# Three batch-1 projections in front of the first attention pass, and a new order in SyncE's queue

## The chip, the cores and the metric

One core of a Trainium2 chip runs the whole program. The metric is device time in microseconds, the median of several executions. TensorE's clock has two levels, 1.2 and 2.4 GHz; the profile gives the granted share of full speed, 0.50 or 1.00.

## The reference

The input is `x` of shape (4, 512, 512): four batches of 512 rows. What is computed, with all else cut:

```
x = x + attention(layernorm(x))        # 32 query heads and 8 key heads of 16 features
x = x + ffn(layernorm(x))              # 1376 hidden features
attention: q, k, v = x@Wq, x@Wk, x@Wv; q, k = rope(q), rope(k)
           probs = softmax(causal(q k^T / 4)); out = (probs v) @ Wo
ffn:       (silu(x @ W_gate.T) * (x @ W_up.T)) @ W_down.T
```

All of it is float32.

## The kernel before

The kernel has two phases. Phase 1 does attention for the four batches, in four passes over one batch each; phase 2 does the rest, mostly the feed-forward matmuls. The change is in phase 1.

**A pass.** Pass `b` has eight groups, one for each key head with its four query heads. A group is numbered `n = 8*b + g` and has four slots, `i` = 0 to 3, for four row tiles or key chunks. In each slot TensorE, by `iteration`, interleaves three things step by step, the steps being `(i, j)`: the transposed scores of group `n` (`scores_t`, L1222), from which ScalarE makes the exponentials (L792); the plain scores of group `n+2` (`scores`, L1188, with a mask matmul at L1195), from which VectorE takes row maxima (L929 and L934) out of a ring of three PSUM banks `ps_s`; and the product of masked probabilities and values (`weighted_v`, L1235). The row maxima are split by GpSimd (L682, L684), transposed by TensorE at the end of slot 0 (`transposed_max`, L1206), copied to `m_t` by ScalarE (L785) and sent by SyncE into two rows of `q_rows` (`stage_max`, L465). The first `scores_t` of the next group waits for that transfer.

**Dense units.** Between these steps TensorE computes the next batch's projections, one unit after another in the PSUM bank `ps_d`. A unit of kind R is one of five projections (k=0 the keys, 1 to 4 the queries) and V is the values; each has four pieces of three matmuls of 512 columns (`project`, L1140). U transposes the values, T transposes the normalised rows of the batch after. Each pass has 40 places for a piece, five in a group, given by `gap(n)`; `UNITS_IN` says at which place a unit starts, and its pieces take consecutive places. `dense_evacuated` counts units read out of their bank. ScalarE copies an R unit to `raw` (`raw_rows`, L729, L730 and L743: three copies for k=0, one for the others), GpSimd rotates it in 20 steps at the slots of `ROPE_SLOT` (L595, L599), ScalarE and GpSimd write the bf16 parts (L753, L610) at `LO_SLOT`, and SyncE stores them to scratch (`store_rotated`, L405 and L409). From there `stage_rows` (six transfers, L452 and L455) loads a group's rows into a ring of six.

**The preamble.** Before pass 0 TensorE computes all projections of batch 0, then the transposes of batch 1, then the plain scores of groups 0 and 1. `transposed_max(0)` stands after the first slot of group 1. VectorE takes these maxima with L934.

**SyncE** issues all its transfers in program order and blocks at each wait. In slot `i` of a group it goes through: a rotated store (when the slot before is in `LO_SLOT`), the rows of group `n+3` (`i` = 0), the maxima of group `n+1` (`i` = 1), the output of group `n-1` (`i` = 2), and in pass 0 a 688 KB copy of a weight matrix within DRAM (`copy_raw`, `i` = 2 and 3).

**The end of phase 1.** In the last pass `LAST_O` gives two outputs `ps_o` to VectorE instead of ScalarE (L986), at slots 26 and 30. In a slot VectorE does this work before that of `LAST_XT` (L979, L901).

## Time and profile before

| what | value |
|---|---|
| median of 3 runs | 773.6 us (773.15 to 775.04) |
| the profiled execution's own time | 772.49 us |
| its span | 770.8 us |
| mean granted TensorE clock | 0.989 |
| TensorE busy | 737.8 us, 96% of the span |
| VectorE, ScalarE, GpSimd busy | 445.2, 333.8, 241.9 us |
| preamble up to the first `scores_t` | 53.4 us |
| phase 2 from | 369.6 us |

The span runs from the first to the last instruction; the execution's own time has 1.7 us more. Matmuls are pipelined, so that a busy TensorE row ends later than its columns do: the distance from start to start is the better measure of a matmul.

### The profile page before, as it was taken

How to read it: one execution, taken by the hardware profiler on the slowest of the kernel's cores; microseconds unless marked ns; L12 is line 12 of the kernel's file. 1: busy time of each engine (PE TensorE's matmuls, PEld its weight loads, DVE VectorE, ACT ScalarE, POOL GpSimd, SP SyncE). 2: the span in 40 equal slices, each digit the busy share in tenths (PEclk: the TensorE clock that was granted, in tenths of full speed). 3: DMA queues.
4: the chain of work that ended last, by engine and by line, in shares of the span. 5: the costliest groups of instructions: out<-in, count | busy, mean ns of one | idle time of the engine just before them, and what ended most of it. 6: DMA issues, size and time to landing. Idle time of an engine off the chain costs nothing.

```text
span 770.8 us, 12186 instructions
## 1 busy us (share of the span) xinstructions
PE 737.8 (96%) x4149; PEld 502.4 (65%) x4164; DVE 445.2 (58%) x1136; ACT 333.8 (43%) x646; POOL 241.9 (31%) x467
## 2 busy tenths in 40 slices
PE   5889999999999999998999999999999999999998
PEld 4645444554444543443788888888888888788886
DVE  6897789888987889997355443234232333231212
ACT  4337678767976778667343222111121111111111
POOL 4257885688658774556000000000000000000000
PEclk9869999999999999999999999999999999999999
DMA  7337587234434455530592103211014020030001
GB/s 272 98 108 250 182 280 239 67 87 125 119 96 130 142 179 151 160 99 29 174 310 72 42 14 118 88 59 51 14 48 142 27 82 27 0 110 1 1 0 55
DMA packets 74759, 81.86 MB, mean 106 GB/s; under 512 B 8864, under 2 KB 58528, under 8 KB 74496
## 3 DMA queue, kind: packets, MB, share of 16 engines
q1 hardware_dynamic: 73408, 79.98, 32.7%
q10 hardware_dynamic: 1296, 1.18, 0.5%
q8 instruction: 30, 0.49, 0.3%
q14 instruction: 25, 0.20, 0.1%
HBM read 57.02 MB, written 33.36 MB: 117 GB/s over the span
## 4 chain that ended last, share of the span: by engine, by line
PE 51%; DVE 0%; issue 0%; DVEq 0%
PE bank L1578 35%; PE ps_y L1630 15%; PE bank L1617 1%; DVE x_in L1560 0%; DVEq L1559 0%
## 5 line engine op out<-in xcount | busy, mean ns | idle before, releaser
L929 DVE CUSTOM_DVE_ANT_0 ps_s<-ps_s,mask_row 128x512 f32<-128x512 f32 (+1 forms) x360 | 192.1, 583 | 36.6 <-PE ps_s L1188 34.0
L792 ACT ACTIVATE probs<-ps_t 128x512 f32<-128x512 f32 (+1 forms) x352 | 178.2, 560 | 68.6 <-PE ps_t L1222 68.3
L1535 DVE TENSOR_TENSOR h<-h,bank 128x512 f32<-128x512 f32 (+1 forms) x44 | 30.2, 687 | 212.8 <-PE bank L1578 211.6
L1188 PE MATMUL ps_s<-k_rows,q_rows 96*128 96x256 bf16 (+3 forms) x512 | 141.0, 309 | 5.7 <-DVE m_raw L929 2.9
L1222 PE MATMUL ps_t<-q_rows,k_rows 98*128 98x512 bf16 (+1 forms) x352 | 126.9, 364 | 4.4 <-DMA q_rows<-m_t 2.4
L240 POOL TENSOR_TENSOR var_eps<-mean_var,eps 128x1 f32<-128x1 f32 x16 | 3.0, 189 | 281.7 <-DVE mean_var L235 281.7
L1473 ACT ACTIVATE h<-bank 128x512 f32<-128x512 f32 (+1 forms) x44 | 26.3, 597 | 145.2 <-PE bank L1578 145.2
L1235 PE MATMUL ps_o<-probs,v_ones 128*32 128x512 f32 (+3 forms) x1024 | 82.0, 438 | 3.4 <-POOL probs L693 1.1
L693 POOL TENSOR_SCALAR_AFFINE_SELECT probs<-probs 128x512 f32<-128x512 f32 x128 | 83.4, 652 | 0.0
L1479 ACT CAST h_hi<-h 128x512 fp32r<-128x512 f32 (+1 forms) x44 | 27.3, 620 | 126.5 <-DVE h L1535 126.5
L1188 PEld LDWEIGHTS ps_s<-k_rows,q_rows 96*128 96x128 bf16 x512 | 48.2, 100 | 47.8 <-DVE m_raw L929 22.3
L1630 PE MATMUL ps_y<-wd_hi,h_hi 128*128 128x512 f32 (+1 forms) x176 | 68.8, 391 | 0.0
L1222 PEld LDWEIGHTS ps_t<-q_rows,k_rows 98*128 98x128 bf16 x352 | 34.2, 98 | 53.1 <-issue 18.3
L1630 PE MATMUL ps_y<-wd_lo,h_hi 128*128 128x512 f32 (+1 forms) x176 | 68.5, 389 | 0.0
L1630 PE MATMUL ps_y<-wd_hi,h_lo 128*128 128x512 f32 (+1 forms) x176 | 68.5, 389 | 0.0
L1235 PEld LDWEIGHTS ps_o<-probs,v_ones 128*32 128x32 f32 x1024 | 27.2, 109 | 43.3 <-issue 30.4
L691 POOL TENSOR_TENSOR carrier<-half 128x1 f32<-128x1 f32 x128 | 26.8, 209 | 89.9 <-ACT probs L792 89.8
L929 DVE DVE_READ_ACCUMULATOR2_ANT m_raw<- 128x1 f32 x360 | 50.3, 140 | 0.0
L1578 PE MATMUL bank<-xt_hi,wg_hi 128*128 128x512 f32 (+1 forms) x128 | 50.0, 390 | 0.0
L1578 PE MATMUL bank<-xt_hi,wg_lo 128*128 128x512 f32 (+1 forms) x128 | 49.9, 390 | 0.0
L1578 PE MATMUL bank<-xt_hi,wu_lo 128*128 128x512 f32 (+1 forms) x128 | 49.9, 390 | 0.0
L1578 PE MATMUL bank<-xt_lo,wu_hi 128*128 128x512 f32 (+1 forms) x128 | 49.9, 390 | 0.0
(167 smaller groups left out, 1366.1 us busy)
## 6 DMA issues: line engine op xcount, KB each, us to landing
scratch_o<-o_sb SPq DMA_DIRECT2D x31, 256.0 KB, 2.4
q_rows<-scratch_q_parts SPq DMA_DIRECT2D x32, 192.0 KB
x_in<-in_x SPq DMA_DIRECT2D x16, 256.0 KB, 4.0
q_rows<-scratch_q_parts SPq DMA_DIRECT2D x32, 128.0 KB
o_in<-scratch_o SPq DMA_DIRECT2D x64, 64.0 KB
inverse<-scratch_inverse SPq DMA_DIRECT2D x64, 64.0 KB
x_res<-in_x SPq DMA_DIRECT2D x16, 256.0 KB, 2.7
out<-x_in SPq DMA_DIRECT2D x16, 256.0 KB, 2.1
```

Of the source, the lines that this page charges most:

```text
L691: nc.gpsimd.tensor_tensor(carrier[:, g % 2, c:c + 1], half[:, 0:1], half[:, 0:1], ALU.add)
L693: nc.gpsimd.affine_select(out=diagonal, in_=diagonal, compare_op=ALU.is_ge, fill=0.0, base=0, pattern=[[0, GROUP], [1, P]], channel_multip ...
L792: nc.scalar.activation(probs[:, g % 2, heads * u:heads * (u + 1), CHUNK_AT[c]:CHUNK_AT[c + 1]], ps_t[:, pos % S_BANKS, 0:heads * CHUNK_N[c ...
L929: taken = nc.vector.tensor_tensor_reduce(out=head, in0=head, in1=mask_row[:, T - width:T], scale=1.0, scalar=LOWEST, op0=ALU.add, op1=ALU. ...
L1188: mm = nc.tensor.matmul(bank[:, place], q_rows[r][0:ROWS, j, P * q:P * (q + 1)], k_rows[r][0:ROWS, 0:width], start=(place == 0), stop=(mas ...
L1222: nc.tensor.matmul(ps_t[:, pos % S_BANKS, 0:heads * width], k_rows[r][:, P * c:P * (c + 1)], q_rows[r][:, heads * u:heads * (u + 1), P * c:T],
L1235: mm = nc.tensor.matmul(ps_o[32 * j:32 * j + 2 * DH, P * c:T], v_ones[:, c, g % NKV, :], probs[:, g % 2, j, CHUNK_AT[c]:CHUNK_AT[c + 1]], ...
L1473: nc.scalar.activation(h[0:m, r], bank[units["gate", f] % BANKS][0:m, :], ACT.Silu).then_inc(silu_done, 1)
L1479: nc.scalar.copy(h_parts[0][0:m, r], h[0:m, r]).then_inc(h_hi_ready, 1)
L1535: nc.vector.tensor_tensor(h[0:m, r], h[0:m, r], bank[units["up", f] % BANKS][0:m, :], ALU.mult).then_inc(h_ready, 1)
L1578: mm = nc.tensor.matmul(out, weights(w, c), moving(m, c), start=(c == 0 and n == 0), stop=(c == chunks - 1 and n == 2))
L1630: mm = nc.tensor.matmul(ps_y[:, t], h_parts[w][0:m, r, P * t:P * (t + 1)], wd[p][0:m, f, :], start=(f == 0 and k == 0), stop=(f == FT - 1 ...
```

## The change

Three of the five R units of batch 1 (k = 0, 1, 2) are computed in the preamble, their twelve pieces between the scores of groups 0 and 1 (`AHEAD_AT`), in the banks `ps_t[2]`, `ps_d` and `ps_o`. Pass 0 keeps R3, R4 and V, whose pieces now take every second place, and U and the T units. ScalarE's copies of the first three units stand in the preamble, the first of them ahead of the first group's maxima; GpSimd does the four key steps of the rotation there. SyncE sends the maxima first at `i` = 1, stores rotated parts one slot later, and loads rows of group `n+4` at `i` = 3 instead of `n+3` at the next `i` = 0. `LAST_O` moves one output from slot 30 to slot 29. `transposed_max(0)` uses `ps_t[0]` and semaphores of its own.

```diff
-        steps = [gap(first + n) for n in range(1 if kind in "TU" else 4)]
+        steps = [gap(first + n) for n in ((0,) if kind in "TU" else range(0, 4 * apart[0], apart[0]) if apart else range(4))]
...
+AHEAD = 3
+AHEAD_AT = {(0, 1, 1): (0, 0), (0, 1, 3): (0, 1), (0, 2, 1): (0, 2), (0, 2, 3): (0, 3),
+            (1, 0, 1): (1, 0), (1, 0, 3): (1, 1), (1, 1, 1): (1, 2), (1, 1, 3): (1, 3),
+            (1, 2, 1): (2, 0), (1, 2, 3): (2, 1), (1, 3, 1): (2, 2), (1, 3, 3): (2, 3)}
+FIRST_UNITS = [("R", 3, 2, 2), ("R", 4, 11, 2), ("V", 0, 19, 2), ("U", 0, 27)]
+UNITS_IN = [FIRST_UNITS + NEXT_T] + [QKV_UNITS + NEXT_T] * (B - 3) + [QKV_UNITS, LAST_UNITS]
...
+FIRST_ROPE = [None] * ROPE_AHEAD + [1, 2, 3, 5, 6, 7, 9, 10, 13, 14, 15, 17, 18, 19, 21, 22]
-LO_SLOT = {7: 0, 13: 1, 16: 2, 23: 3, 27: 4}
+LO_SLOT = [{1: 0, 9: 1, 13: 2, 21: 3, 25: 4}] + [{7: 0, 13: 1, 16: 2, 23: 3, 27: 4}] * (B - 2)
-LAST_O = {26: 5, 30: 6}
+LAST_O = {26: 5, 29: 6}
...
-                    if has_next and slot - 1 in LO_SLOT:
-                        store_rotated(sp, b + 1, LO_SLOT[slot - 1])
-                    if i == 0 and n + 3 < GROUPS:
-                        stage_rows((n + 3) // NKV, (n + 3) % NKV, n + 3)
+                    if n == 0 and i == 0:
+                        stage_rows(0, 3, 3)
                     if i == 1 and n + 1 < GROUPS:
                         stage_max(n + 1)
+                    if has_next and slot - 2 in LO_SLOT[b]:
+                        store_rotated(sp, b + 1, LO_SLOT[b][slot - 2])
                     if i == PV_EVACUATE and n >= 1:
                         store_o(b, g - 1)
+                    if i == 3 and n + 4 < GROUPS:
+                        stage_rows((n + 4) // NKV, (n + 4) % NKV, n + 4)
...
             store_rotated(act, 0, 3)
+            raw_rows(1, 0, r_unit(1, 0))
             rotated_top(0, 4)
             first_max_high()
             max_evacuate(0)
             store_rotated(act, 0, 4)
+            for k in range(1, AHEAD):
+                raw_rows(1, k, r_unit(1, k))
...
                     for j in range(GROUP):
                         scores(0, n, i, j)
+                        if (n, i, j) in AHEAD_AT:
+                            k, piece = AHEAD_AT[n, i, j]
+                            dense(1, "R", k, r_unit(1, k), piece)
                     if (n, i) == (1, 0):
                         transposed_max(0)
```

## Rows read from the trace of the kernel before

**Rows 1.** The page: busy time by engine, and the chain that ended last.
```profile
PE 737.8 (96%) x4149; PEld 502.4 (65%) x4164; DVE 445.2 (58%) x1136; ACT 333.8 (43%) x646; POOL 241.9 (31%) x467
...
PE bank L1578 35%; PE ps_y L1630 15%; PE bank L1617 1%; DVE x_in L1560 0%; DVEq L1559 0%
```

**Rows 2.** Busy time by stretch (microseconds, instructions), clock, DMA share, GB/s: preamble.
```profile
40.50:46.90 6.40, 6.15 (x27) 2.89 (x29) 5.62 (x10) 1.14 (x2) 6.01 (x7) 0.50 0.50 139
46.90:50.40 3.50, 2.53 (x14) 0.89 (x14) 3.34 (x8) 1.40 (x3) 0.99 (x1) 0.99 0.02 7
50.40:53.70 3.30, 3.30 (x16) 1.76 (x17) 3.14 (x7) 0.00 (x0) 0.00 (x0) 0.50 0.77 219
```

**Rows 3.** The same view with the same columns, pass 0.
```profile
53.40:133.80 80.40, 77.22 (x558) 39.50 (x564) 66.72 (x218) 59.59 (x121) 57.73 (x108) 1.00 0.69 228
```

**Rows 4.** Timeline of the preamble: start, duration, instruction, idle time before it.
```profile
40.53 0.61 PE L1188 MATMUL ps_s<-k_rows,q_rows 96*128 96x512 bf16 x1 [1.48 <-DMA q_rows<-scratch_q_parts]
...
46.81 1.04 ACT L753 COPY r_top<-rot 128x1024 bf16<-128x1024 bf16 x1 [3.75 <-POOL rot L599]
...
48.74 0.22 PE L1206 MATMUL ps_d<-ident_b,m_parts 128*128 128x128 bf16 x1
...
53.36 0.58 PE L1222 MATMUL ps_t<-q_rows,k_rows 98*128 98x512 bf16 x1
```

**Rows 5.** Timeline: one piece of R0, the matmul after it, ScalarE's copies of R0.
```profile
54.25 0.58 PE L1140 MATMUL ps_d<-xt_hi,w_hi 128*128 128x512 f32 x1
...
55.13 0.39 PE L1222 MATMUL ps_t<-q_rows,k_rows 98*128 98x512 bf16 x1
...
60.25 0.59 ACT L729 ACTIVATE raw<-ps_d 64x512 f32<-64x512 f32 x1 [0.27 <-PE ps_d L1140]
...
61.47 0.58 ACT L743 COPY raw<-ps_d 128x512 f32<-128x512 f32 x1
```

**Rows 6.** Timeline: transposed maxima of four groups, in pass 0 and pass 2.
```profile
77.40 0.23 PE L1206 MATMUL ps_t<-ident_b,m_parts 128*128 128x128 bf16 x1
...
88.04 0.23 PE L1206 MATMUL ps_t<-ident_b,m_parts 128*128 128x128 bf16 x1
...
286.53 0.22 PE L1206 MATMUL ps_t<-ident_b,m_parts 128*128 128x128 bf16 x1
...
294.28 0.22 PE L1206 MATMUL ps_t<-ident_b,m_parts 128*128 128x128 bf16 x1
```

**Rows 7.** Timeline: a group's maxima in `m_t`, SyncE's transfer, the matmul that waited.
```profile
77.72 0.25 ACT L785 CAST m_t<-ps_t 32x128 bf16<-32x128 f32 x1 [0.38 <-PE ps_t L1206]
...
81.97 0.67 SPq L465 DMA_DIRECT2D q_rows<-m_t  x1
...
84.87 0.39 PE L1222 MATMUL ps_t<-q_rows,k_rows 98*128 98x512 bf16 x1 [0.32 <-DMA q_rows<-m_t]
```

**Rows 8.** Waits of TensorE for the maxima, 53 to 370 us (total, times, longest).
```profile
PE ps_t L1222 <- DMA q_rows<-m_t: 2.4, 4, 1.3
```

**Rows 9.** The same wait within pass 0, 56.7 to 136.9 us.
```profile
PE ps_t L1222 <- DMA q_rows<-m_t: 1.0, 2, 0.7
```

**Rows 10.** VectorE's groups by shape, 57 to 133 us: busy us, mean ns.
```profile
L896 DVE TENSOR_SCALAR xn<-x_in,mean_var,rstd 128x512 f32<-128x512 f32 x4 | 4.1, 1015 | 0.0
```

**Rows 11.** Timeline of the end of phase 1.
```profile
361.45 0.86 PE L1235 MATMUL ps_o<-probs,v_ones 128*32 128x256 f32 x16
...
363.94 0.69 DVE L901 TENSOR_TENSOR xt_lo<-ps_s,xt_hi 128x512 fp32r<-128x512 f32 x1
364.55 0.68 DVE L986 COPY o_sb<-ps_o 128x512 f32<-128x512 f32 x1
...
365.38 2.36 PE L1235 MATMUL ps_o<-probs,v_ones 128*32 128x512 f32 x32 [1.11 <-POOL probs L693]
...
369.60 0.47 PE L1578 MATMUL bank<-xt_hi,w_hi 128*128 128x512 f32 x1 [1.86 <-PEq L260]
```

**Rows 12.** DMA issues of the whole run: size, median microseconds to landing.
```profile
scratch_wg_raw<-in_wg SPq DMA_DIRECT2D x4, 688.0 KB, 6.1
```

More of the change, by code:

```diff
@@ L66, in pieces_at @@
     at, done = {}, {}
-    for place, (kind, k, first) in enumerate(units):
-        steps = [gap(first + n) for n in range(1 if kind in "TU" else 4)]
+    for place, (kind, k, first, *apart) in enumerate(units):
+        steps = [gap(first + n) for n in ((0,) if kind in "TU" else range(0, 4 * apart[0], apart[0]) if apart else range(4))]
         for piece in range(4):
@@ L78 @@
               ("T", 3, 39)]
-UNITS_IN = [QKV_UNITS + NEXT_T] * (B - 2) + [QKV_UNITS, LAST_UNITS]
-PRE_DENSE = KC + N_ROPE + 2 + KC
-PRE_UNITS = PRE_DENSE + 1
+AHEAD = 3
[4 more added lines that the diff above has]
+UNITS_IN = [FIRST_UNITS + NEXT_T] + [QKV_UNITS + NEXT_T] * (B - 3) + [QKV_UNITS, LAST_UNITS]
+PRE_DENSE = KC + N_ROPE + 2 + KC + AHEAD
 PRE_BANKS = 1 + S_BANKS
-UNIT0 = [PRE_UNITS + sum(len(u) for u in UNITS_IN[:b]) for b in range(B)]
-ROPE_SLOT = [3, 4, 5, 6, 7, 8, 10, 10, 11, 12, 13, 14, 15, 17, 18, 19, 21, 22, 23, 25]
+UNIT0 = [PRE_DENSE + sum(len(u) for u in UNITS_IN[:b]) for b in range(B)]
+ROPE_AHEAD = 4
+FIRST_ROPE = [None] * ROPE_AHEAD + [1, 2, 3, 5, 6, 7, 9, 10, 13, 14, 15, 17, 18, 19, 21, 22]
+ROPE_SLOT = [FIRST_ROPE] + [[3, 4, 5, 6, 7, 8, 10, 10, 11, 12, 13, 14, 15, 17, 18, 19, 21, 22, 23, 25]] * (B - 2)
 KEY_STEPS, PAIR_STEPS = 4, 8
@@ L312, in dense_bank @@
         def dense_bank(unit):
-            if isinstance(unit, int) and unit < PRE_DENSE and unit % PRE_BANKS:
+            if unit == PRE_DENSE - 1:
+                return ps_o[:]
+            if unit < PRE_DENSE and unit % PRE_BANKS:
                 return ps_t[:, unit % PRE_BANKS - 1]
@@ L676, in _ @@
                     rotated_low(0, REST_STEP.index(s))
+            for s in range(ROPE_AHEAD):
+                rotate(1, s)
+                if s in REST_STEP:
+                    rotated_low(1, REST_STEP.index(s))
             def split_max(n):
@@ L708, in iteration @@
                     if has_next:
-                        for s, at in enumerate(ROPE_SLOT):
+                        for s, at in enumerate(ROPE_SLOT[b]):
                             if at == slot:
@@ L780, in max_evacuate @@
                 if n == 0:
-                    act.wait_ge(dense_ready, PRE_UNITS)
-                    nc.scalar.copy(m_t[0][:], ps_d[rows, 0:P]).then_inc(dense_evacuated, 1)
+                    act.wait_ge(first_max_ready, 1)
+                    nc.scalar.copy(m_t[0][:], ps_t[rows, 0, 0:P]).then_inc(first_max_evacuated, 1)
                 else:
@@ L826, in iteration @@
                         max_evacuate(n + 1)
-                    if i == PV_EVACUATE and n >= 1 and (has_next or slot not in LAST_O):
+                    if i == PV_EVACUATE and n >= 1 and (has_next or g - 1 not in LAST_O.values()):
                         o_evacuate(b, g - 1)
                         if g == 0:
-                            v_place(b, UNIT0[b - 1] + 6 if b else KC + N_ROPE + 1)
+                            v_place(b, v_unit(b))
                     for u in range(GROUP // HEADS_OF[i]):
@@ L835, in iteration @@
                                 dense_read(b, *done[slot, j])
-                    if has_next and slot in LO_SLOT:
-                        rotated_top(b + 1, LO_SLOT[slot])
+                    if has_next and slot in LO_SLOT[b]:
+                        rotated_top(b + 1, LO_SLOT[b][slot])
                     if not has_next and (slot - CTX_HI) % TT == 0 and 0 <= slot - CTX_HI < TT * TT:
@@ L998, in next_work @@
                     if slot in NEXT_XT:
-                        work.append(lambda: xt_low(b + 2, NEXT_XT[slot], UNIT0[b] + len(QKV_UNITS) + NEXT_XT[slot]))
+                        work.append(lambda: xt_low(b + 2, NEXT_XT[slot], UNIT0[b + 1] - KC + NEXT_XT[slot]))
                 return work
@@ L1200, in transposed_max @@
                 if n == 0:
-                    bank_free(PRE_UNITS - 1, 0)
-                    to, ready = ps_d[:], dense_ready
+                    pe.wait_ge(dense_evacuated, KC + N_ROPE + 2 + KC)
+                    to, ready = ps_t[:, 0], first_max_ready
                 else:
@@ L1217, in scores_t @@
                 pos = T_AT[c] + u
+                if n == 0 and c == 0 and j == 0:
+                    pe.wait_ge(dense_evacuated, PRE_DENSE - AHEAD + 1)
                 if c == 0 and j == 0:
@@ L1269, in _ @@
                         mm.then_inc(dense_ready, 1)
-            for unit in range(KC, PRE_DENSE):
+            for unit in range(KC, PRE_DENSE - AHEAD):
                 kind, k, of = ("R", unit - KC, 0) if unit < KC + N_ROPE else (
```

16 lines of the change are left out of this document (13 added, 3 removed).

## The prediction

> **What bounds the kernel now.** I read the page first, then busy time by stretch, then the timeline around the preamble, then the waits. The page gives TensorE 96% of the span, and the chain that ended last is TensorE all through phase 2 [rows 1]; phase 2 isn't touched and moves as a block. In pass 0 TensorE is busy 77.2 of 80.4 us, VectorE 66.7, ScalarE 59.6 [rows 3]: TensorE sets the pace, with VectorE close behind. The preamble is the exception. From the first score at 40.53 to the first transposed score at 53.36 [rows 4] it lasts 12.8 us. Counted from the code, the two groups stream 2 x 7,168 = 14,336 columns, which is 6.0 us at 2.4 GHz. Twice that passes for two reasons that the stretches show [rows 2]: until 46.9 the clock is at 1.2 GHz (0.50), and after it rises VectorE is busy 3.34 of 3.50 us while TensorE is busy only 2.53; then the clock is back at 0.50 to 53.7. There is room for matmuls here; in pass 0 there is hardly any.
>
> **The price of a piece.** A piece of three matmuls takes 55.13 - 54.25 = 0.88 us from its start to the next bf16 matmul [rows 5]. The other pieces of pass 0 have the same pattern, some a tenth shorter, so I take 0.86. Twelve pieces are 10.3 us at full clock.
>
> **Preamble, TensorE.** The new preamble holds 6.0 + 10.3 = 16.3 us of full-clock work. The stretch to 46.9 at 1.2 GHz begins the same way, and the pieces make TensorE denser in it, so I let the clock rise at the same place: 6.4 us at half speed add 3.2. Later I let it stay up, as TensorE no longer waits for VectorE; VectorE's 12.1 us of work in the three stretches [rows 2] fits below. One new wait comes from ScalarE's queue. Unit R0 ends at about 49.7: the first slot's 2,560 columns at 1.2 GHz end at 42.6; the second's 2,048 and two pieces, mostly at 1.2 GHz, at 47.2; the third's 1,536 and two pieces at full clock take 2.4 more. Then ScalarE copies it three times, 61.47 + 0.58 - 60.25 = 1.8 us [rows 5], to 51.7; `rotated_top(0, 4)`, ready since 46.8, takes its 1.04 behind that [rows 4], to 52.7; only then come the first maxima's high part, VectorE's low part (another 0.6), and `transposed_max(0)` at about 53.3 instead of 48.74 [rows 4]. TensorE is there at about 52.9, and VectorE, which stands at the low part, has three banks to make up. I charge 0.9 us; 0 if R0 ends sooner, 2 if VectorE's arrears count in full. Sum 16.3 + 3.2 + 0.9 = 20.4, against 12.8: **+7.6 us** (6.5 to 9.5).
>
> Hidden in the preamble: GpSimd's four key steps and one low part start after 52.7; seven of its instructions of these kinds took 6.01 us [rows 2], so five take less, and TensorE ends at about 61; ScalarE's copies of R1 and R2 are 0.6 each, the last just after R2's last piece, where the first exponential has to wait for the first transposed score (0.58 [rows 4]) anyway. Behind ScalarE's store of k=4 stand its copies of R1 and R2, which wait for GpSimd's steps 0 and 1, done before R1 ends at about 56.6. If this cover went, a late copy of R2 would hold the first exponential and the bank of R3.
>
> **Pass 0, TensorE.** Twelve pieces go: **-10.3 us** (9.4 at 0.78 each, 10.6 at 0.88). What is left costs the same, at every second place or not, since each piece stands alone between bf16 matmuls already.
>
> **Pass 0, VectorE.** Without a wait TensorE would need 80.4 - 10.3 - 1.0 = 69.1 us, and VectorE has 66.7. So it is a race. Between the transposed maxima at 77.40 and 88.04 [rows 6] lie four pieces: 10.64 - 4 x 0.86 - 0.32 = 6.9 us for a group without pieces. But the group from 286.53 to 294.28, which has none, takes 7.75: there VectorE sets the pace. Over eight groups VectorE has 8.3 us each and TensorE 8.6, but the `xn` instructions (1.0 us each, four of them [rows 10]) fall into two groups, where VectorE comes to about 8.9. I charge 2.0 us for the pass, a quarter of a microsecond a group. Bounds: 0, if the three banks between the two even it all out; 3.4, if it can't be busier than in the preamble's 92% (12.1 of 13.2 us [rows 2]): 66.7/0.92 = 72.5.
>
> **SyncE's order.** The maxima are in `m_t` at 77.97, but SyncE issues them at 81.97, behind the rotated store and six row loads, and TensorE waits 0.32 [rows 7]. There are four such waits in TensorE's row, 2.4 us [rows 8], 1.0 of it in pass 0 [rows 9]. With the maxima first at `i` = 1, what stands ahead of them is row loads issued from `i` = 3, two slots or some 4.5 us earlier; between 77.97 and 81.97 SyncE had six such loads and the end of a store to issue, so six take less than 4 us [rows 7]. So all four go: **-1.0** in pass 0, **-1.4** later. Bounds: 0 and 2.4, plus some tenths where idle time is too short to be listed. Past the maxima are moved five rotated stores a pass (six transfers for the keys, three each for the others, the largest under 4 us of issue by the same comparison). The one that could be missed is k=2: stored at slot 18, and the first group of the next batch is loaded at slot 19, so SyncE stands there until it lands. The maxima are next due at slot 21, two slots or 4 us later, and are only wanted at slot 24: nothing. In pass 0 a 688 KB copy takes 6.1 us to land [rows 12] and is now issued behind the row loads, right ahead of the maxima. Issued some 2 us before them, it could hold them for another 4 us; the first matmul that waits comes 84.87 - 77.97 = 6.9 us after `m_t` [rows 7]. So this too is hidden, by little.
>
> On this the Trainium skill, page "DMA: Bandwidth & Descriptors", section "Queues, rings and completion order", says that each DMA engine takes the descriptors of a ring in order. By that rule the copy goes ahead of the maxima in full, which is the 4 us charged here; were they free to pass it, the sum would be the same, since both are hidden.
>
> **The end of phase 1.** TensorE's last product starts at 365.38, after an idle 1.11 us [rows 11]. The page blames a mask, but VectorE's copy of the output before it ends at 365.23 and stands behind `xt_lo`, which ends at 364.63. What it copies was complete at about 362.3 [rows 11]. At slot 29 it goes ahead of that pair, and the product can start at about 364.2: **-1.1 us** (0 to -1.2). The handover to phase 2, up to 369.60, hangs on it.
>
> **Sum.** +7.6 - 10.3 + 2.0 - 1.0 - 1.4 - 1.1 = **-4.2 us**. Against the profiled execution's own 772.5 that is 768.3; that execution was 1.1 below the median of 773.6, so the forecast is **769.4 us**. What a measurement can tell from no change is 0.3%, 2.3 us: faster means under 771.3.
>
> **Rivals.**
> - *VectorE becomes the bound of pass 0* (0.20). It has 66.7 of some 70 us, and ScalarE 59.6. Against it: groups now at 9 us with VectorE fully busy lose only tenths. With the 3.4 bound and 0.6 more for ScalarE: 769.4 + 2.0 = 771.4.
> - *The clock falls once more* (0.12). After 46.9 it fell when TensorE was busy 2.53 of 3.50 us [rows 2]; the new wait at `transposed_max(0)` and VectorE's arrears could do the same. A stretch of 3.3 us at 0.50, as the one to 53.7, costs 1.7: 771.1. Against it: with pieces, TensorE would be idle under 1 us in such a stretch. The Trainium skill, page "TensorE: Matmul & The Clock Gate", section "A second HAM failure mode: psum-queue depth-cycling", has the clock swing when TensorE idles briefly and often between groups of matmuls while it cycles through banks. The trace agrees with the fall at 50.4; by that rule the time would be this rival's.
> - *The waits for the maxima stay* (0.08), through the copy or the row loads: no -2.4, 771.8.
> - *Cheaper preamble* (0.10): no wait at `transposed_max(0)`, and no loss to VectorE: 769.4 - 2.9 = 766.5.
> - *Slower: the clock stays at 1.2 GHz through the preamble* (0.05). Then 14,336 + 18,432 columns take 27.3 us, with 2.4 of overhead and 0.5 of waiting 30.2, which is +17.4 instead of +7.6: 779.2. It decides when the low stretch gets 8.4 us longer (0.5 each), to about 55.3. Against it: the clock rose at 46.9 with less work in flight.
>
> The forecast itself has 0.45, with 767.4 to 771.2 as its own range. From the cases: faster by over 0.3% 0.75 (the forecast, the cheap one, and over half of the near rivals, which stand at the edge), within 0.3% 0.19, slower 0.06. The range takes in all but the slow case and the far ends of the others: 765.8 to 773.0.
>
> **What would show it.** The first L1222 at about 61 instead of 53.4 (preamble); the clock at 1.00 from 46.9 on; L1206 of group 0 near 53.3 with idle time before the next scores; pass 0 in about 71.1 us instead of 80.4, VectorE busy over 93%; no wait of L1222 for `m_t`; phase 2 starting at about 365.4 instead of 369.6. The prediction falls if the preamble grows by 10 us or more, if pass 0 stays above 74, or if loads of rows appear among TensorE's waits.

## The result and the profile after

The changed kernel took 777.3 us in the median, the kernel before, measured beside it, 773.1: ratio 1.0056, 95% interval 1.004 to 1.0071. It is slower, by 4.3 us, where 4.2 less was forecast. Of its 22 executions 21 took 771.8 to 782.2 us; one took 3527 us and is not in the ratio. The profiled execution took 774.7 us and has a span of 773.0, against 772.5 and 770.8 before.

Four places divide both traces alike: the first transposed score (L1254 after, L1222 before), the first one of pass 1, the last transposed maxima, the first matmul of phase 2.

| us | before | after | change | forecast |
|---|---|---|---|---|
| up to the first transposed score | 53.36 | 61.35 | +8.0 | +7.6 |
| pass 0 | 80.4 | 77.5 | -2.9 | -9.3 |
| passes 1 to 3, to the last transposed maxima | 219.6 | 218.0 | -1.6 | -1.4 |
| from there to phase 2 | 16.24 | 15.11 | -1.1 | -1.1 |
| first matmul of phase 2 at | 369.60 | 371.91 | +2.3 | -4.2 |

Three steps out of four came out within half a microsecond. Pass 0 is 6.4 us off, and that alone turns the sign. The trace shows +2.3 us in all, the median +4.3; the other 2 us lie in executions that no trace was taken of. Two things are on record about them. The time goes with the mean granted clock: the fastest of the 21 had 0.996, the slowest (782.2 us) 0.983. And that isn't all of it, since the eight others at 0.989 to 0.991 took 776.5 us on average, and the profiled one, at 0.990, took 774.7.

The view by stretch, with the columns of [rows 2]: two stretches of the new preamble, and pass 0, which answers to [rows 3].

```profile
51.00:54.80 3.80, 2.03 (x11) 0.94 (x11) 3.73 (x6) 0.29 (x2) 3.64 (x3) 0.97 0.17 46
54.80:57.90 3.10, 3.10 (x12) 2.10 (x11) 1.51 (x4) 0.59 (x1) 1.46 (x3) 0.50 0.69 205
...
61.35:138.84 77.49, 69.28 (x522) 33.53 (x529) 64.29 (x217) 56.01 (x117) 52.07 (x103) 1.00 0.73 234
```

TensorE lost 8 us of work in pass 0 (69.3 busy, 77.2 before) and took only 2.9 less to do it: it stands idle 8.2 us of the pass instead of 3.2. VectorE, busy 83%, is no fuller than before. The forecast's own sign of failing, a pass 0 above 74 us, has come. What TensorE waits for is in the view of its waits, 61 to 139 us, which answers to [rows 9]:

```profile
PE ps_t L1254 <- DMA q_rows<-m_t: 5.2, 4, 2.1
PE ps_o L1269 <- ACT o_sb L829: 0.9, 1, 0.9
PE ps_s L1218 <- DVE m_raw L959: 0.7, 2, 0.3
```

The waits for the maxima, which the new order of SyncE was forecast to end, grew from 1.0 to 5.2 us. One of them, in the timeline of the kernel after (m_t is the maxima's copy by ScalarE, L486 their transfer, L455 a copy of weights, L426 the rotated store, L473 and L476 the row loads); it answers to [rows 7]:

```profile
67.51 0.57 SPq L455 DMA_DIRECT2D scratch_wg_raw<-in_wg  x1
68.19 2.53 SPq L426 DMA_DIRECT2D scratch_k_parts<-r_top  x4
70.76 1.17 SPq L426 DMA_DIRECT2D scratch_k_parts<-r_low  x2
72.04 0.76 SPq L473 DMA_DIRECT2D k_rows<-scratch_k_parts  x1
...
72.93 0.26 ACT L812 CAST m_t<-ps_t 32x128 bf16<-32x128 f32 x1 [0.30 <-PE ps_t L1236]
...
75.44 0.57 SPq L455 DMA_DIRECT2D scratch_wg_raw<-in_wg  x1
76.48 0.68 SPq L486 DMA_DIRECT2D q_rows<-m_t  x1
...
80.50 0.39 PE L1254 MATMUL ps_t<-q_rows,k_rows 98*128 98x512 bf16 x1 [1.57 <-DMA q_rows<-m_t]
```

SyncE spends 3.7 us on the six transfers of a rotated store, then 3.4 on six row loads, then issues a copy, and only then the maxima, 3.3 us after they were ready at 73.19. They are used 4.0 us later. Without the wait of 1.57 us the matmul would have started at 78.93, so 3.3 + 4.0 us met a slack of 5.7. When the copy ahead of the maxima landed is in the DMA view of that one issue:

```profile
L455 SPq DMA_DIRECT2D scratch_wg_raw<-in_wg x1: 574/574/574, 75.4 to 75.4; - x1
...
DMA to landing us min/median/max: 5.0/5.0/5.0
```

75.44 + 5.0 = 80.4: the 8 KB of maxima are there when the 688 KB copy in front of them is. (The view has no landing of the maxima themselves; the matmul that waited for them stands for it.) The other three waits are alike: copies issued at 93.70, 103.69 and 125.51 took 5.9, 5.8 and 4.5 us and landed at 99.6, 109.5 and 130.0; the matmuls that waited start at 99.81, 109.39 and 130.11. The forecast drew on the Trainium skill here, page "DMA: Bandwidth & Descriptors", section "Queues, rings and completion order": each DMA engine takes the descriptors of a ring in order. All four waits agree with that, and with what the forecast drew from it, that the copy goes ahead in full.

In the preamble, the timeline of the kernel after shows why the first transposed maxima start at 52.34 with TensorE idle before them:

```profile
49.87 1.05 ACT L780 COPY r_top<-rot 128x1024 bf16<-128x1024 bf16 x1
50.82 0.22 ACT L800 CAST m_parts<-m_raw 128x16 bf16<-128x16 f32 x1
50.99 1.26 POOL L618 TENSOR_TENSOR rot<-raw,cos 128x512 f32<-128x512 f32 x1 [2.60 <-ACT r_top L780]
51.07 1.22 DVE L971 TENSOR_TENSOR m_parts<-m_raw,m_parts 128x16 bf16<-128x16 f32 x1 [1.22 <-ACT m_parts L800]
...
52.34 0.23 PE L1236 MATMUL ps_t<-ident_b,m_parts 128*128 128x128 bf16 x1 [1.20 <-DVE m_parts L971]
```

A step of VectorE on 16 columns takes 1.22 us: it ends with the rope step (GpSimd's rotation) that began 0.08 us before it. And the end of phase 1, which answers to [rows 11]: the output is out of the way at 366.5, and the last product starts without idle time.

```profile
365.81 0.69 DVE L1016 COPY o_sb<-ps_o 128x512 f32<-128x512 f32 x1
...
367.63 2.40 PE L1269 MATMUL ps_o<-probs,v_ones 128*32 128x512 f32 x32
...
371.91 0.47 PE L1615 MATMUL bank<-xt_hi,w_hi 128*128 128x512 f32 x1 [1.88 <-PEq L269]
```

### The profile page after: what moved, and what is told of

The parts are those of the page before. It is cut to its first block, busy times and chain, and to the rows that moved or that the text cites. A ratio compares the mean times of both kernels' runs of the same rounds, so it can differ in the third digit from the quotient of the medians.

```text
span 773.0 us, 12187 instructions
## 1 busy us (share of the span) xinstructions
PE 737.4 (95%) x4149; PEld 502.0 (65%) x4164; DVE 443.9 (57%) x1136; ACT 332.7 (43%) x646; POOL 242.4 (31%) x467
## 4 chain that ended last, share of the span: by engine, by line
PE 51%; DVE 0%; issue 0%; DVEq 0%
PE bank L1615 35%; PE ps_y L1667 15%; PE bank L1654 1%; DVE x_in L1597 0%; DVEq L1596 0%
## 5 line engine op out<-in xcount | busy, mean ns | idle before, releaser
L1218 PE MATMUL ps_s<-k_rows,q_rows 96*128 96x256 bf16 (+3 forms) x512 | 138.6, 305 | 4.3 <-DVE m_raw L959 2.7
L1254 PE MATMUL ps_t<-q_rows,k_rows 98*128 98x512 bf16 (+1 forms) x352 | 126.7, 364 | 7.4 <-DMA q_rows<-m_t 5.2
L1254 PEld LDWEIGHTS ps_t<-q_rows,k_rows 98*128 98x128 bf16 x352 | 34.1, 98 | 57.7 <-issue 20.6
L959 DVE DVE_READ_ACCUMULATOR2_ANT m_raw<- 128x1 f32 x360 | 50.6, 141 | 0.0
```

Of the source, the lines that this page charges most:

```text
L959: taken = nc.vector.tensor_tensor_reduce(out=head, in0=head, in1=mask_row[:, T - width:T], scale=1.0, scalar=LOWEST, op0=ALU.add, op1=ALU. ...
L1218: mm = nc.tensor.matmul(bank[:, place], q_rows[r][0:ROWS, j, P * q:P * (q + 1)], k_rows[r][0:ROWS, 0:width], start=(place == 0), stop=(mas ...
L1254: nc.tensor.matmul(ps_t[:, pos % S_BANKS, 0:heads * width], k_rows[r][:, P * c:P * (c + 1)], q_rows[r][:, heads * u:heads * (u + 1), P * c:T],
```

## The experiments

The columns: the ratio to the kernel before, measured beside it, with its interval; from each run's trace the first transposed score, the stretch from the transposed maxima of group 1 to those of pass 1's group 1 ("pass 0 stretch", in which 10 of the 12 pieces were), TensorE's waits for the maxima in pass 0, and the start of phase 2. Runs e1 to e4, e5 to e8, e9 to e12 and e13 to e16 shared a chip and their runs of before (772.8, 772.5, 773.1 and 773.1 us). A trace is of one execution, which need not be the median one: e3's took 767.3 us against a median of 771.2, e7's was the slowest of twelve, 779.5 against 774.4; the others lie within 3 us.

| kernel | ratio | first scores | pass 0 stretch | waits | phase 2 |
|---|---|---|---|---|---|
| before | 1 | 53.36 | 80.24 | 1.0 | 369.60 |
| after | 1.0056 (1.004 to 1.0071) | 61.35 | 78.70 | 5.2 | 371.91 |
| e1 after, SyncE's old order | 1.007 (1.0046 to 1.0094) | 59.45 | 82.27 | 5.6 | 375.53 |
| e2 before, SyncE's new order | 0.9982 (0.9964 to 0.9999) | 52.46 | 79.38 | 0 | 366.05 |
| e3 after, copies in pass 1 | 0.9985 (0.9959 to 1.001) | 58.00 | 73.83 | 0 | 364.40 |
| e4 after, stores at `i`=1 | 0.9964 (0.9942 to 0.9986) | 58.63 | 74.25 | 0.3 | 364.83 |
| e5 e4, ScalarE's maxima first | 0.993 (0.9909 to 0.9952) | 56.84 | 74.18 | 0.2 | 362.77 |
| e6 e5, with fillers | 0.9912 (0.989 to 0.9933) | 55.39 | 74.09 | 0 | 361.21 |
| e7 before, with fillers | 1.0029 (1.0012 to 1.0047) | 53.40 | 85.49 | 4.6 | 374.95 |
| e8 before, last output | 0.997 (0.9955 to 0.9984) | 51.94 | 80.25 | 0.8 | 365.96 |
| e9 after, small copies | 0.9978 (0.996 to 0.9997) | 61.75 | 73.93 | 0 | 369.08 |
| e10 e5, thin pieces | 0.989 (0.9866 to 0.9914) | 56.93 | 72.05 | 0.5 | 361.14 |
| e11 e6, P times V in three | 0.998 (0.9961 to 0.9998) | 55.07 | 75.95 | 1.1 | 366.37 |
| e12 e5, every place | 0.9944 (0.9925 to 0.9962) | 55.67 | 75.90 | 0 | 363.26 |
| e13 e5, half maxima | 0.9905 (0.9875 to 0.9935) | 58.26 | 72.93 | 0 | 362.81 |
| e14 e13, thin pieces too | 0.988 (0.9854 to 0.9905) | 55.90 | 72.27 | 0.8 | 359.95 |
| e15 after, with fillers | 1.0019 (0.9993 to 1.0044) | 59.51 | 79.72 | 5.2 | 370.85 |
| e16 before, e2 and e8 together | 0.9953 (0.9935 to 0.997) | 53.68 | 79.42 | 0 | 366.85 |

### Is it SyncE's order? (e1, e2)

e1 gives SyncE back its old order everywhere in the kernel after; e2 has the new order alone, in the kernel before, by this edit:

```diff
-                    if has_next and slot - 1 in LO_SLOT:
-                        store_rotated(sp, b + 1, LO_SLOT[slot - 1])
-                    if i == 0 and n + 3 < GROUPS:
-                        stage_rows((n + 3) // NKV, (n + 3) % NKV, n + 3)
+                    if n == 0 and i == 0:
+                        stage_rows(0, 3, 3)
                     if i == 1 and n + 1 < GROUPS:
                         stage_max(n + 1)
+                    if has_next and slot - 2 in LO_SLOT:
+                        store_rotated(sp, b + 1, LO_SLOT[slot - 2])
...
+                    if i == 3 and n + 4 < GROUPS:
+                        stage_rows((n + 4) // NKV, (n + 4) % NKV, n + 4)
```

> The changed kernel with SyncE's order of before in all passes (rotated store one slot after, rows of group n+3 at slot 0); the three projections in front, the spread places and the last-output slot stay. Theory A (in pass 0 SyncE sends the maxima late, behind a rotated store, six row loads and a 688 KB copy, and TensorE waits for them): TensorE's waits for the maxima in pass 0 fall from 5.2 us to under 1.5, pass 0 (first transposed score to that of pass 1) from 77.5 to 73 or less, and the kernel is at 0.993 to 0.999 of before. Theory B (VectorE and ScalarE have no room in a denser pass 0): the waits only change their name, pass 0 stays above 76, the time stays at 1.004 or more. Theory C (the longer preamble is what costs): the same as B, with the preamble at 20 to 21 us.

> The kernel before with SyncE's new order alone (maxima first, rotated stores two slots after, rows of group n+4 at slot 3). Theory A: its rotated stores stand mostly at slots 1 of a group (9, 25, 29) or 2 (18), one at 3 (15), so only one group of pass 0 has a store, rows and a copy ahead of its maxima; waits for the maxima of 1 to 3 us in pass 0, none in passes 1 and 2; 0.997 to 1.001 of before. If the copies alone make the maxima late (theory D: they land late because a 688 KB copy is issued just ahead), most groups of pass 0 wait and the time is 1.002 to 1.006.

The order as such is good. Without it the changed kernel is no better (five waits for the maxima, 7.8 us in all, 5.6 of them in pass 0, where under 1.5 were expected), and in the kernel before it ends every one of them, where 1 to 3 us were expected to stay, and gives 1.4 us (0.1 to 2.8). So the order does what the forecast said with the rotated stores where they were, and not with the ones that the change moved: `LO_SLOT` of pass 0 is 1, 9, 13, 21, 25, and two slots later is `i` = 3 for all five, right ahead of the row loads.

e1's trace also shows that such a wait can cost more than its length. Around its longest, 2.8 us, the view by stretch (columns as above) has:

```profile
75.50:79.50 4.00, 1.51 (x16) 0.26 (x8) 1.71 (x6) 0.50 (x2) 3.92 (x8) 1.00 1.03 339
79.50:86.30 6.80, 6.51 (x20) 2.87 (x24) 3.83 (x11) 3.62 (x7) 2.17 (x4) 0.50 0.48 172
```

TensorE was busy 1.51 of 4.00 us, and then its clock is at 0.50 for 6.8 us. At half speed that is up to 3.4 us more, on top of the wait, where e1's stretch is 3.6 us longer than the changed kernel's. In the trace of the changed kernel no clock fell in pass 0; whether it does in the executions with the lower mean clock is not shown.

### Two ways to take the delay out (e3, e4)

e3 issues the twelve copies of weights at the same places of pass 1 instead of pass 0. e4 leaves them, and SyncE stores pass 0's rotated tiles four slots after `LO_SLOT`, behind the maxima:

```diff
-                    if not positive(b) and i >= 2 and g < 6:
+                    if b == 1 and i >= 2 and g < 6:
```
```diff
-                    if has_next and slot - 2 in LO_SLOT[b]:
-                        store_rotated(sp, b + 1, LO_SLOT[b][slot - 2])
+                    late = 2 if b else 4
+                    if has_next and slot - late in LO_SLOT[b]:
+                        store_rotated(sp, b + 1, LO_SLOT[b][slot - late])
```

> The changed kernel with the twelve 688 KB weight copies in pass 1 instead of pass 0. Theory D (the copies make the maxima land late): waits for the maxima in pass 0 fall from 5.2 us to under 1, new ones may come in pass 1; time at 0.995 to 1.000. Theory A with the issue queue as its main part: SyncE saves only 1.2 us of issue a group, the maxima still go out 1 to 3 us late, and some 2 to 3 us of waits remain: 1.000 to 1.003. Theory B: no change, 1.005.

> The changed kernel with the rotated stores of pass 0 issued four slots after ScalarE's part instead of two, so behind the maxima at slot 1 of a group and not ahead of the row loads at slot 3. Theory A (issue queue): the maxima go out 1.9 us earlier in four groups, waits in pass 0 fall from 5.2 us to 1 to 3; time 0.999 to 1.003. Theory D: the copies still stand just ahead of the maxima, waits stay above 3.5 us; 1.003 to 1.005. Theory B: 1.005.

Each alone ends the waits in pass 0, but for 0.3 us, and shortens its stretch by 4.9 and 4.5 us (in e3 a wait of 1.45 us turns up in pass 1, where the copies went). In the timeline of e4 the maxima go out 0.02 us after they are ready, and the store follows them:

```profile
70.20 0.26 ACT L813 CAST m_t<-ps_t 32x128 bf16<-32x128 f32 x1 [0.30 <-PE ps_t L1237]
70.48 0.66 SPq L486 DMA_DIRECT2D q_rows<-m_t  x1
71.24 2.52 SPq L426 DMA_DIRECT2D scratch_k_parts<-r_top  x4
73.80 1.60 SPq L426 DMA_DIRECT2D scratch_k_parts<-r_low  x2
```

The copies stand where they stood. With the maxima issued at most 1.1 us late in any group of pass 0, they cost 0.3 us of waiting. The time came out better than either theory had it (0.999 at best): the first scores too are 2.7 us sooner than in the changed kernel, with nothing in the edit to bring it. In e4's trace the preamble's first low stretch of the clock ends at 40.7 us instead of 44.4, and the second one is missing. In e3's the first is 3.4 us long instead of 10.2, and the second is missing too. So the start of phase 2 holds more than the edit, and the stretch and the waits are the better witness.

### Issued late, or landing late? (e9)

e9 keeps twelve copies at their places in the kernel after, each of an eighth of its rows, and sends the rest in pass 1:

```diff
+                few = rows // 8
-                at = slice(rows * (n % 4), rows * (n % 4 + 1))
+                at = slice(rows * (n % 4), rows * (n % 4) + few) if first else slice(rows * (n % 4) + few, rows * (n % 4 + 1))
...
-                    if not positive(b) and i >= 2 and g < 6:
-                        copy_raw(2 * g + i - 2)
+                    if b < 2 and i >= 2 and g < 6:
+                        copy_raw(2 * g + i - 2, b == 0)
```

> The kernel after, with pass 0's twelve copies of weights issued at the same places, but each of an eighth of its rows (86 KB in place of 688 KB); the other seven eighths follow in pass 1. SyncE issues as many DMAs as before in pass 0. Theory A, that the maxima are issued late: a copy issued ahead of them costs SyncE its 0.6 us whatever its size, so the late issues stay (2 to 4 us behind m_t), and most of the 5.2 us of waits: time at 775 to 777. Theory D, that the maxima land late behind 688 KB in the queues: the landing falls from 4 to 5.5 us to about 2.5, the waits go, and the time comes to the 771 us of the run in which the copies are all in pass 1. Between the two: 773.

Timeline of e9, the place of the wait shown above:

```profile
73.33 0.26 ACT L813 CAST m_t<-ps_t 32x128 bf16<-32x128 f32 x1 [0.30 <-PE ps_t L1237]
...
75.72 0.57 SPq L456 DMA_DIRECT2D scratch_wg_raw<-in_wg  x1
76.75 0.70 SPq L487 DMA_DIRECT2D q_rows<-m_t  x1
...
79.25 0.10 PEld L1255 LDWEIGHTS ps_t<-q_rows,k_rows 98*128 98x128 bf16 x1 [0.62 <-DMA q_rows<-m_t]
```

The maxima are issued as late as in the kernel after (3.2 us behind `m_t` here, 1.8 to 2.8 at four other groups), but are there in 2.5 us instead of 4.0. The load of their rows as weights waits 0.6 us, but under TensorE's own work, and no matmul of pass 0 waits (two do in pass 1, 2.3 us, beside the seven eighths). e9 also thins the traffic as a whole (139 GB/s in the mean from 60 to 140 us, against 229), so by itself it doesn't tell the copy just ahead from the load at large. e4 has a cleaner case: in pass 2, with no copy near, a group's maxima are issued 3.0 us late (ready at 267.65, issued at 270.69), and no matmul waits. So lateness of the issue alone is hidden, by e9 and e4; a 688 KB copy near the maxima alone is all but hidden, by e4; the two together are not. Theory A's "the waits stay whatever the copy's size" is refuted, and so is landing alone as the cause.

### The preamble and the clock (e5, e6, e7, e15)

e5 is e4 with ScalarE's last steps of the preamble in another order; e6, e7 and e15 add matmuls whose result nobody uses (fillers) to e5, to the kernel before and to the kernel after, 29 of 512 columns behind three of the preamble's units.

```diff
             rotated_top(0, 3)
             store_rotated(act, 0, 3)
-            raw_rows(1, 0, r_unit(1, 0))
             rotated_top(0, 4)
             first_max_high()
+            raw_rows(1, 0, r_unit(1, 0))
```
```diff
+            def keep_busy(count):
+                for _ in range(count):
+                    nc.tensor.matmul(ps_o[:], ident_b[:], mask_q[:].rearrange("p j t -> p (j t)"), start=True, stop=True)
...
+                keep_busy({KC + N_ROPE: 12, KC + N_ROPE + 1: 3, PRE_DENSE - AHEAD - 1: 14}.get(unit, 0))
```

> As the run in which SyncE stores pass 0's rotated tiles four slots late, with one more edit: in the preamble ScalarE copies r_top and first_max_high's part ahead of raw_rows of the next unit, so that VectorE's last reduction for the first maxima runs before GpSimd's rope step begins. Theory that VectorE's small step was held up by GpSimd: it falls from 1.22 us to about 0.17, the first transposed maxima start 1.5 to 2.9 us sooner (the copies gone ahead of it, and the held step), PE's idle stretch behind 51 us is gone, and the first pass begins 1 to 2.5 us sooner; time 1 to 2.5 us below the run it is built on. Rival, that TensorE's projection units in front of the pass set its begin whatever the maxima do: the transposed maxima start sooner and the first scores don't; no change in the time.

> As e5, with 29 matmuls of 512 columns added in the preamble where TensorE stood idle (12 behind the V unit, 3 behind the U unit, 14 behind the last unit of keys), their results not used. Theory that the half clock of the preamble costs time: the granted clock stays at 1.00 from the first units on, the units that ran at 1.2 GHz (10 to 13 us long in the other runs) take half their time, less the fill itself; the first scores 1 to 3 us sooner and the time 1 to 3 us below e5. Rival, that the fill takes PE's time where it was wanted: the preamble grows by up to 29 times 0.216 us = 6.3 us less the idle time that it lies in, and the time is level or up to 3 us above.

> The kernel before with the same 29 matmuls in its preamble, as a control of e6. If the clock is what they change, the gain over the kernel before is like e6's over e5 (0 to 3 us), since the low stretch of the kernel before is about as long. If not, no change or up to 3 us slower.

> The kernel after with the 29 filler matmuls in its preamble and nothing else. If the second fall of the clock (1.2 GHz from 54.8 to 57.9 us) costs what its length says, 1.5 us, and the first low stretch was already over at 44.8, the first scores come 1 to 2 us sooner and the time falls by 1 to 2 us, to about 775.5. If the held step of VectorE (1.22 us) and ScalarE's queue set the begin whatever the clock, no change; if the fill is in the way, up to 2 us more.

Timeline of e5:

```profile
48.64 0.22 ACT L801 CAST m_parts<-m_raw 128x16 bf16<-128x16 f32 x1 [1.06 <-DVE m_raw L965]
...
49.12 0.17 DVE L972 TENSOR_TENSOR m_parts<-m_raw,m_parts 128x16 bf16<-128x16 f32 x1
...
50.34 0.23 PE L1237 MATMUL ps_t<-ident_b,m_parts 128*128 128x128 bf16 x1
```

With no rope step beside it VectorE's step is back at 0.17 us, and TensorE goes from one matmul to the next without idle time. The first scores come 1.8 us sooner than in e4, and the ratio goes from 0.9964 to 0.993; the two were measured in different sessions and their intervals overlap, but the traces say the same. (The transposed maxima start 0.9 us sooner than in e4, where 1.5 to 2.9 were expected.) All six kernels with the old order of ScalarE and three projections in front have the 1.22 us (after, e1, e3, e4, e9, e15), and all others 0.17 or 0.18. The Trainium skill, page "SBUF — State Buffer", section "Who interferes with whom", says that a VectorE instruction with two inputs in SBUF shares a read interface with GpSimd and is shut out while GpSimd holds it. The 1.22 and 0.17 us agree with that.

The clock: e6 shows 1.00 over the whole of its preamble, and its first scores are another 1.5 us sooner; its 1.1 us of median lie inside both intervals. The kernel after falls to 0.50 at 54.6 for 3.4 us, behind its idle stretch (TensorE busy 2.03 of 3.80). What that fall costs can be read from kernels in which it is missing. e15, the kernel after with fillers further ahead:

```profile
51.00:55.00 4.00, 2.33 (x13) 1.40 (x14) 4.00 (x7) 0.25 (x1) 3.76 (x4) 1.00 0.27 68
55.00:59.50 4.50, 4.50 (x26) 2.86 (x24) 2.60 (x5) 0.58 (x1) 1.87 (x2) 1.00 0.48 141
```

From the first transposed maxima to the first scores it takes 59.51 - 52.10 = 7.4 us, the kernel after 61.35 - 52.34 = 9.0. So the second fall costs 1.6 us. But it isn't the fillers that stop it: e1, e3 and e4 have none, and in their traces too the clock stays up and the way takes 7.4 us, while e9 falls like the kernel after and takes 9.0. In all six the 3.8 us around the held step are alike, with TensorE busy 2.02 or 2.03; what decides it stays open.

e15's ratio is 1.0019 against 1.0056, and the waits for the maxima are 5.2 us in both: the kernel isn't faster than before with the preamble's clock mended. In e15 a wait of 2.4 us in pass 0 has a fall behind it as in e1 (TensorE busy 1.35 of 3.80 us, then 0.50 for 3.4), so that its stretch is 1.0 us longer than the changed kernel's.

In the kernel before, the fillers bring nothing (e7): the first low stretch shrinks from 13.6 to 3.4 us (44.4 to 47.8), the clock falls again at 51.3 for 3.4 as before, and the first scores come at 53.40. That VectorE sets this preamble ([rows 2]: 3.34 of 3.50 us busy) fits, but no run shows it. The pass behind it has 4.6 us of waits for the maxima instead of 1.0 and one more fall of the clock, in the slowest of its twelve executions. With the old order the traces have 1.0 (before), 0.8 (e8) and 4.6 us: why they differ wasn't found.

### The end of phase 1 (e8), and what the three projections bring (e16)

e8 has `LAST_O = {26: 5, 29: 6}` and its condition alone, e16 this and e2's edit, with no projection moved.

> The kernel before with the change's last edit alone: the output of the last group but one is written at slot 29 in place of 30, ahead of the last group's. By the forecast's step for the end of phase 1: phase 2 begins 0.9 to 1.1 us sooner after the last transposed maxima (369.60 minus 353.36 = 16.2 us before), the wait of 1.11 us at the last P times V gone; time 1.0 us less, ratio about 0.9987, at the bound of what is measured. Rival, that phase 2's first bank or a transfer sets its begin: the wait goes and phase 2 begins no sooner.

> The kernel before with SyncE's new order and the earlier last output, and no projection moved. Alone they gave 0.9982 and 0.9970. If they add up, 0.995, about 769.3, which is level with the change whose pass-0 stores are late (0.9964): then moving three projections in front is worth nothing by itself until the preamble's held step is mended. If the three projections carry the gain, this run stays at 0.998.

In e8 the wait of 1.11 us is gone from TensorE's list and phase 2 begins 15.11 us after the last transposed maxima, as in the kernel after: the mechanism and its 1.1 us are right. The ratio gives 2.3 (1.2 to 3.5), of which the trace explains 1.1. In e16 the two edits add up (0.9982 x 0.997 = 0.9952, measured 0.9953). e16 shows what is left for the main part of the change: 0.9953 without it, 0.9964 with it in e4's order, 0.993 in e5's. So three projections in front brought nothing that can be told until ScalarE's order was put right, and then some 1.8 us, which isn't settled either: the intervals overlap, and the runs are from different sessions.

### Why pass 0 doesn't gain more (e10 to e14)

In e5 the pass takes 73.0 us, between the places of the first table; the forecast had 71.1. Five edits look for the rest. e10 leaves out two of the three matmuls of each piece of pass 0, e13 takes VectorE's masked maxima there over half of the keys only, and e14 does both. e11 breaks up TensorE's longest block of P times V (probabilities times values), and e12 puts the pieces of pass 0 at every place instead of every second.

```diff
e10:                for n, (w, x) in enumerate(PRODUCTS):
+                    if thin and n > 0:
+                        continue
e11:
-PV_AT = {(1, 1): (-1, (2, 3)), (3, 3): (0, (0, 1))}
+PV_AT = {(0, 1): (-1, (1,)), (1, 1): (-1, (2, 3)), (3, 3): (0, (0,))}
e12:
-FIRST_UNITS = [("R", 3, 2, 2), ("R", 4, 11, 2), ("V", 0, 19, 2), ("U", 0, 27)]
+FIRST_UNITS = [("R", 3, 2), ("R", 4, 11), ("V", 0, 19), ("U", 0, 27)]
e13, e14:
+                            few = width // 2 if 2 <= n < NKV + 2 else width
+                            head = bank[:, width * (j + 1) - few:width * (j + 1)]
```

> The best order so far without the filler matmuls (e5), and each of the twelve pieces that are left in pass 0 has one matmul in place of three: hi times hi alone, so the projections of batch 1 lack their low parts. Its time shows what a piece taken out of pass 0 is still worth there. If TensorE sets pass 0's pace, 24 matmuls less are 12 x 0.86 x 2/3 = 6.9 us off pass 0, and the time is 6 to 7 us below e5. If it is the alternation of VectorE and TensorE that sets it (VectorE stands 1.5 us a group while TensorE is at the P times V block), pass 0 gets only 1 to 3 us shorter.

> e6 (ScalarE's maxima first, with filler matmuls) with one more edit: in all passes P times V of tile 1 is moved from slot i=3, where it stands behind tile 0's, to the first place of the next group, so that TensorE's longest block without scores is 0.9 us and not 1.7. If the blocks starve VectorE (1.49 us of its idle time lies in one, in each group), then each of 32 groups where VectorE sets the pace gains up to 0.8 us: 5 to 20 us. If VectorE only makes up in one place what it loses in another, or if the exponentials wait for the transposed scores instead, no change within 2 us; a new wait for ps_o's evacuation would make it slower.

> e5 with the projections left in pass 0 at every place instead of every second, from the same first places. The forecast held that the spacing costs and saves nothing, as each piece stands alone between bf16 matmuls either way: within 1 us of e5. Rival: closer pieces starve VectorE and ScalarE in the groups that hold four of them, and the groups without any don't give it back: 1 to 3 us slower.

> e5 (SyncE's stores four slots late, ScalarE's maxima first) with VectorE's masked maxima of pass 0 taken over the last half of the keys only, so the maxima there are of fewer scores. 12 instructions a group are 0.13 to 0.27 us shorter each, some 2.4 us a group, 19 us in the pass, at the same number of matmuls. If VectorE holds TensorE back in pass 0 (the race that the forecast priced at 2.0 us and that seems to cost 3.9), the pass falls from 74.2 us by 3 to 5 us, to the 69 to 71 that TensorE needs. If ScalarE's exponentials or TensorE's own order set the pace, it stays within 1 us.

> The shorter maxima together with the pieces of one matmul in three. With three matmuls a piece VectorE's side alone was worth what e13 shows; with it gone, 24 matmuls less should be worth their full time, 6.9 us off e13 (5.7 in the stretch from group 1 to group 1). If ScalarE (56 us busy in the pass) or the waits for GpSimd's low parts come next, 3 us or less.

- e10: all 24 matmuls left out lie in the stretch (e14's expectation counts too few there), 6.9 us by the price of a piece, and the stretch gets 2.1 shorter. TensorE alone isn't the bound.
- e13: VectorE is busy 50.6 instead of 65.5 us in the stretch, which gets 1.25 shorter. Nor is VectorE alone; 3 to 5 us were expected of that theory, and it fell.
- e14: both together give 1.9 in the trace, where 24 matmuls alone were expected to give 5.7 more. One fall of the clock is in that:

```profile
103.90:107.30 3.40, 3.40 (x24) 1.98 (x17) 0.85 (x5) 1.60 (x4) 1.80 (x4) 0.50 0.87 282
```

It costs up to 1.7 us, so the two edits together are worth 1.9 to 3.6. That is still far from 6.9. What TensorE waits for more is GpSimd, whose low part of the maxima comes behind its other work (rope steps and masks); e10 has 2.5 us of that already. The waits in the stretch, of e14 and then of e5:

```profile
PE ps_t L1240 <- POOL m_parts L712: 3.0, 4, 1.7
PE ps_o L1273 <- ACT o_sb L830: 0.8, 3, 0.3
```
```profile
PE ps_t L1237 <- POOL m_parts L712: 0.8, 2, 0.6
PE ps_s L1219 <- DVE m_raw L960: 0.7, 2, 0.3
```

- e11: the theory that the long block of P times V starves VectorE fell. The timeline has one block of 16 matmuls in e6, and two of 8 in e11:

```profile
168.75 1.71 PE L1270 MATMUL ps_o<-probs,v_ones 128*32 128x512 f32 x16
170.40 0.39 PE L1255 MATMUL ps_t<-q_rows,k_rows 98*128 98x512 bf16 x1
```
```profile
171.04 1.06 PE L1270 MATMUL ps_o<-probs,v_ones 128*32 128x512 f32 x8
...
172.03 0.39 PE L1255 MATMUL ps_t<-q_rows,k_rows 98*128 98x512 bf16 x1
...
173.01 0.85 PE L1270 MATMUL ps_o<-probs,v_ones 128*32 128x384 f32 x8
173.79 0.50 PE L1171 MATMUL ps_d<-xt_hi,w_hi 128*128 128x512 f32 x1
```

One block takes 1.65 us to the next matmul, the two 0.99 + 0.78 = 1.77. Most groups got slower, those of passes 1 to 3 by up to 0.4 us: 5.3 us in all by the two ratios.
- e12: the spacing that the forecast costed at nothing is worth 1.7 us in the stretch (75.90 against 74.18); the ratios, 0.9944 against 0.993 in different sessions, go the same way without settling it.

## Why the prediction was wrong

- **Preamble** (+7.6, measured +8.0). Right in sum, and by luck; the parts were otherwise. The clock rose sooner (at 44.4, not 46.9), the transposed maxima were a microsecond early (52.34, forecast 53.3), and against that the clock fell once more, the rival with 0.12, for 1.6 us. The argument against that rival, TensorE idle "under 1 us in such a stretch", failed: it was idle 1.8 of 3.8. Kernels with the same preamble and other clocks had +4.6 to +8.4 (e3, e9). The step "VectorE's low part (another 0.6)" took 1.22, for a reason the forecast didn't see. (In the rival "Slower", 2.4 us of overhead would be 2.6 by the forecast's own price of a piece.)
- **SyncE's order** is the step that failed: "So all four go: -1.0 in pass 0", and "this too is hidden, by little". In passes 1 to 3 it held (-1.4 forecast, -1.6 measured, no wait left). In pass 0 it took two delays one at a time against the same 6.9 us of slack. The slack itself was read too large: the 6.9 held a wait of 0.32, and it was of a group with its pieces still in. In the changed kernel three of the four groups that waited had 5.7 us from `m_t` to the matmul, and one 6.7. The row loads were said to be done, since they are issued "two slots or some 4.5 us earlier"; the copy was charged 4 us from an issue in time. But the stores that the change moves to `i` = 3 put 3.7 us ahead of the loads in one group and 1.9 in others, so that the maxima were issued 3.3 us late, and the copy's 4 us came on top. In after's first wait: 3.3 + 4.0 us, of which 1.6 stuck out. The charge for the copy was right there to a tenth (4.0 to 5.5 us in the other three); the queue that the moved stores join was listed only for the maxima they pass, not for the loads in front of which they come to stand. +4.2 instead of -1.0: 5.2 of the 6.4 us, confirmed by e3, e4 and e9, which give back 4.5 to 4.9 in the stretch. The rival "the waits stay" priced them at the old 2.4 us; none had them grow, and none had the clock fall behind them, as it did in e1 and e15.
- **Pass 0, VectorE**: the race was there, and mis-sized. With no waits for the maxima (e5) pass 0 is 7.4 us shorter than before, so 10.3 + 1.0 - 7.4 = 3.9 us went to it, where 2.0 were charged, with 3.4 as the bound. (In the kernel after it is 77.5 - 5.2 - 69.1 = 3.2, the other 1.2 of the 6.4 us.) The bound was VectorE's alone; by e10, e13 and e14 neither TensorE nor VectorE alone holds the pass, and the waits for GpSimd grow, from 0.8 to 2.5 us (e10) and 3.0 (e14), when TensorE has less to do. None of the three others is 90% busy beside TensorE, which in e5 is at 97% of the stretch. Which engine holds which group stays open.
- **The end of phase 1** (-1.1) was right, place and size, by trace and by e8 and after alike.
- Together: with the one step right, e4 comes to 0.9964 against a forecast of 0.9946 (769.4 of 773.6), inside its interval. Part of that is luck: in e4's trace the preamble adds 5.3 us instead of 7.6, by its clock, and pass 0 gives 7.4 instead of 9.3.

The fastest version that computes everything is e6, 765.8 us, 0.9912 (0.989 to 0.9933): the change, stores four slots late in pass 0, ScalarE's maxima first, and fillers; e5 without fillers is 766.9, and the two can't be told apart.

## What to carry to other kernels

When a change moves an issue on an in-order queue, write out that queue for a whole group, transfer by transfer, with what it now stands in front of as well as what it passes; and add up every delay that draws on the same slack before calling any of them hidden. A small transfer that the bound engine waits for should not be issued behind a large one: put it in front, or cut the large one. A rival that says "the wait stays" needs a price for the wait growing too, and for what the clock does behind it. And one trace is one execution: before a ratio is put down to an edit, see that the two traces have the same clock where the edit changes nothing.

## What the runs showed of the hardware

- Four times a matmul that waited for 8 KB of maxima started within 0.2 us of the end of the 688 KB copy issued before them, 4.5 to 5.9 us after that copy's issue; behind 86 KB they were there in 2.5 us from their own issue.
- A VectorE instruction on 16 columns took 1.22 us beside a rope step of GpSimd (both inputs of each in SBUF), and 0.17 without one.
- Behind the same 3.8 us, with TensorE busy 2.02 or 2.03, the clock fell to 0.50 in two traces (after, e9) and stayed at 1.00 in four (e1, e3, e4, e15). The way from the first transposed maxima to the first scores took 9.0 us in the two and 7.4 in the four.
- Behind a wait of TensorE in pass 0 the clock was at 0.50 for 6.8 us in e1 (wait 2.8 us) and for 3.4 in e15 (wait 2.4); behind waits of 1.6 and 2.1 us in the kernel after it stayed at 1.00.
- 29 matmuls without use in the preamble had the clock at 1.00 up to the first scores in e6, where e5 is at 0.50 from 33.3 to 43.4; the first transposed maxima come 1.45 us sooner (48.89 against 50.34). In the kernel before (e7) they left 3.4 us at 0.50 of the first 13.6, and the first scores came no sooner.
- Splitting a block of 16 matmuls of P times V in two cost 0.12 us at the block itself, and up to 0.4 us in a group of passes 1 to 3.
